# GpSimd's additions to the output wait for one more event of TensorE: the transposes behind the held-weight up product

## What is computed

```python
confidences = sigmoid(einsum('bsh,eh->bse', x, conf_w) + conf_b)
top_bids, selected_experts = top_k(confidences * wealth, 2)
combine = sum(one_hot(selected_experts, 8) * softmax(top_bids)[..., None], axis=2)
g = einsum('bsh,ih->bsi', x, gate_w)        # per expert, i = 1024
u = einsum('bsh,ih->bsi', x, up_w)
expert_out = einsum('bsi,hi->bsh', silu(g) * u, down_w)
output = einsum('ebsh,bse->bsh', expert_out, combine)
x = x + tanh(g_ffn) * output
```

## Time and profile before

| | |
|---|---|
| median of 3 runs | 1449.71 us |
| the profiled execution | 1448.41 us |
| its span, first to last instruction | 1446.8 us |
| mean granted TensorE clock | 0.987 of full speed |
| TensorE busy (matmul) | 1358.9 us, 94% |
| VectorE, ScalarE busy | 1018.4 us, 933.8 us |
| chain that ended last | TensorE 36% of the span, DMA 2% |

### The profile page before, as it was taken

How to read it: one execution, slowest core, us unless ns; L and a number is a source line. 1 busy time by engine, 2 the same in 40 slices (tenths; PEclk the granted TensorE clock), 3 DMA queues, 4 the chain that set the end, 5 groups by cost and what they waited for, 6 DMA issues and landing times. The chain is left out here.

```text
span 1446.8 us, 41651 instructions
## 1 busy us (share of the span) xinstructions
PE 1358.9 (94%) x13880; PEld 971.7 (67%) x13880; DVE 1018.4 (70%) x2553; ACT 933.8 (65%) x1940; POOL 485.5 (34%) x655
## 2 busy tenths in 40 slices
PE   2999999999999999999999958999999999999996
PEld 1466666666666666666666646887777787777774
DVE  4688888888888888888888875666546663444442
ACT  5677878787887878787887765666656553333331
POOL 4423232433433333434432143333344333222221
PEclk9999999999999999999999968999999999999998
DMA  4010101111111101111100335433376743221461
GB/s 118 27 41 26 42 26 36 41 40 47 39 48 32 54 30 45 42 33 54 38 28 21 114 112 156 115 96 90 87 207 185 234 138 89 32 34 31 118 201 16
DMA packets 54867, 107.16 MB, mean 74 GB/s; under 512 B 10833, under 2 KB 32721, under 8 KB 54673
## 3 DMA queue, kind: packets, MB, share of 16 engines
q0 software_dynamic: 23712, 55.71, 14.9%
q1 hardware_dynamic: 30112, 47.75, 10.5%
q10 hardware_dynamic: 848, 1.07, 0.3%
HBM read 69.16 MB, written 35.34 MB: 72 GB/s over the span
## 5 line engine op out<-in xcount | busy, mean ns | idle before, releaser
L875 ACT ACTIVATE sg<-gP,consts 128x512 f32<-128x512 f32 x126 | 86.5, 686 | 242.9 <-PE uP L1436 242.5
L1353 DVE SCALAR_TENSOR_TENSOR act_h<-uP,consts,sg 128x512 f32<-128x512 f32 x126 | 94.5, 750 | 207.5 <-ACT sg L875 207.1
L1436 PE MATMUL fP<-zTs,ws 128*128 128x112 f16 (+1 forms) x1536 | 221.1, 294 | 7.8 <-DVE zTs L1320 5.2
L987 DVE CUSTOM_DVE_ANT_0 ms<-simP,madd,sim_undo 112x488 f32<-112x488 f32 x256 | 184.0, 719 | 5.0 <-remote 2.5
L1436 PE MATMUL fP<-ws,zTs 128*128 128x512 f16 x768 | 186.8, 379 | 0.5 <-DVE kT L977 0.2
L733 ACT ACTIVATE pr<-ms,nmax 112x488 f32<-112x488 f32 x256 | 179.0, 699 | 4.6 <-DVE nmax L987 1.5
L993 DVE SCALAR_TENSOR_TENSOR pT<-ptP,pT 122x448 f16<-122x448 f32 x256 | 157.5, 615 | 28.8 <-ACT pT L740 28.0
L1436 PE MATMUL yP<-W,aT 128*128 (+1 forms) x1512 | 175.4, 273 | 1.7 <-DVE aT L1359 1.7
L1436 PEld LDWEIGHTS fP<-zTs,ws 128*128 128x128 f16 x1536 | 109.8, 99 | 99.6 <-issue 36.8
L1436 PEld LDWEIGHTS yP<-W,aT 128*128 128x128 f16 x1512 | 147.6, 98 | 33.0 <-issue 3.3
L740 ACT ACTIVATE pT<-ptP 122x448 f16<-122x448 f32 x256 | 137.8, 538 | 41.2 <-PE ptP L1494 37.7
(11 more groups left out here) (220 smaller groups left out, 2502.7 us busy)
## 6 DMA issues: line engine op xcount, KB each, us to landing
raw<-wffn POOLq DMA_DIRECT2D x36, 512.0 KB, 6.1
split_experts<-W POOLq DMA_DIRECT2D x12, 1024.0 KB
W<-split_experts SPq DMA_DIRECT2D x16, 768.0 KB
xc<-ctxt SPq DMA_DIRECT2D x32, 375.0 KB
xt<-routed_rows POOLq DMA_DIRECT2D x63, 129.0 KB, 2.5
raw<-wffn SPq DMA_DIRECT2D x12, 512.0 KB, 5.3
xl<-x SPq DMA_DIRECT2D x32, 112.0 KB
xres<-x SPq DMA_DIRECT2D x32, 112.0 KB
```

What stands on the lines that cost most here:

```text
L875: nc.scalar.activation(sg[i][:, :], gP[i][:, :], ACT.Silu, scale=constant(place, 0)).then_inc(s_silu, 1)
L987: nc.vector.tensor_tensor_reduce(out=ms[h % 2][:, :], in0=simP[h % 2][0:S, 0:NK], in1=madd[p][:, :], scale=sim_undo[0:S, 0:1], scalar=3.0e ...
L1353: nc.vector.scalar_tensor_tensor(out=act_h[i][:, :], in0=uP[i][:, :], scalar=constant(place, 2), in1=sg[i][:, :], op0=ALU.mult, op1=ALU.mu ...
L1436: last = nc.tensor.matmul(o, lhs(k, a), rhs(k, c), start=n == 0, stop=n == len(todo) - 1)
```

## The change

One more wait in `add_tile`, between the wait for ysb and the addition. For every tile but the last, the addition of tile t also waits for the transposes of the second half of the activation of tile t + 1 (turned(t + 1, 1) is t + 2, the count of s_at behind them). These come in TensorE's tile t + 2, right behind the up product with weights held; ysb of tile t is written at the beginning of the same tile t + 2.

```diff
@@ -619,6 +619,8 @@
             def add_tile(t, k):
 
                 pool.wait_ge(s_yw, t + 1)
+                if t < NT - 1:
+                    pool.wait_ge(s_at, turned(t + 1, 1))
                 apart(pool)
                 pool.indirect_dma_start(out[:, :], bass.IndirectOffsetOnAxis(ap=xt[k][:, D:D + 1].bitcast(I32), axis=0),
                                         ysb[t % 2][:, :], None, compute_op=ALU.add).then_inc(s_add, 16)
```

## The result

The changed kernel takes 1472.29 us in the median of 4 runs (1470.16 to 1474.61), against 1450.22 for the kernel before (4 runs), a ratio of 1.0162 [1.0149, 1.0176]: 22 us longer. Lines of kernel.py behind the edit stand two further down (L623 is L625 now, L875 is L877).

The account below looks back on a forecast made before the run. TensorE was taken to lead nearly always in the expert stage. 18.3 us for the late power plus 7.4 for raw pieces, 25.7, on the profiled 1448.41 gave 1474.1; the median being 1.3 higher, 1475 us was forecast, range 1461 to 1486.

Parts of the forecast that it names:

- Size and sign: Whole kernel: slower, by 25.7 us, to 1475 us; 0.88 for slower by over 0.2%.
- The addition 2.7 us later: GpSimd's addition in tile 11 would start at 971.98 instead of 969.26, behind the transposes.
- Plain tiles and tail cost nothing: Tiles without raw pieces or a power, and the end, hide the wait entirely: cost 0.
- First cost: Power for the next expert's scale, 2.7 us late, delays the silu and lengthens tiles: seven experts, 18.3 us.
- Squares of pieces 4 and 5 hidden under the power: Late squares one tile before the late power overlap with it; the pair costs the larger, not the sum.
- Second cost: Squares of raw pieces 0 to 2, 2.5 us late, less ScalarE's idle before silu: 7.4 us over six experts.
- The upper bound, neighbours adding (37 us): If late neighbouring tiles added instead of overlapping, the whole cost would be about 37 us.
- The rival of the port: VectorE's two-input residual holds each pair's first raw issue, six times 0.7 us more: 1479 us, chance 0.05.
- The 0.2 us: Moved additions no longer start under VectorE's splits and shorten, making raw pieces 2.5 instead of 2.7 us late.
- GpSimd as the bound: Additions landing after 8.6 us overrun GpSimd's round, 0.6 us in perhaps ten tiles: 1481 us, chance 0.04.
- A faster held-weight product: TensorE's held-weight product speeds up without GpSimd's work beside it, at most 19 us: 1431 us, chance 0.07.
- What the profile would show: Additions 4.4 us into a tile, raw-piece wait up from 21.9 to about 50 us, long tiles twice per expert.

Follow-up runs that it names:

- wait_elsewhere: Kernel before plus the added wait only in steps with nothing urgent queued behind the addition (33 additions); 1446.33 us, ratio 1.0012.
- wait_raw_first: Changed kernel with only the raw issues moved to the head of GpSimd's step, the power left behind; 1462.03 us, 1.0088 of the kernel before.
- wait_before_power: Kernel before plus the added wait only on the seven additions whose landing the power waits for; 1461.80 us, ratio 1.0110.
- wait_power_first: Changed kernel with only the power moved to the head of GpSimd's step, raw issues left behind; 1465.16 us, 1.0094 of the kernel before.
- wait_work_first: Changed kernel with raw issues and power both moved to the head of GpSimd's step; 1439.90 us, 0.9966 of the kernel before.
- later_work_first: Kernel before plus a wait for the tile's second up product, raw issues and power at the step's head; 1454.35 us, ratio 1.0035.
- later_wait: Changed kernel with the wait moved to the end of the tile's second up product; 1554.79 us, 1.0725 of the kernel before.
- before_again: The kernel before, unchanged, run once more for a second trace; 1449.99 us.
- work_first_no_wait: Kernel before, without the added wait, raw issues and power moved to the head of GpSimd's step; 1447.47 us, ratio 0.9985.
- idle_wait: Kernel before plus the same wait instruction for an event one tile earlier, always past, so nothing is delayed; 1449.94 us, ratio 1.0004.
- idle_work_first: Kernel before plus the wait that delays nothing, raw issues and power at the head of GpSimd's step; 1447.77 us, ratio 0.9989.
- wait_before_raw: Kernel before plus the added wait only in the steps that issue raw pieces behind the addition; 1460.74 us, ratio 1.0107.

## Why the prediction was right, and where not

**Size and sign** were right: 1475 forecast, 1472.3 measured, 25.7 us of cost forecast and 25.2 in the trace. That the two agree so closely is in part luck: by the medians the cost is 22.1, against the second trace of the kernel before 23.6, and 3.5 us of it are half clock and -2.4 the plain tiles, both in no step of the sum. Not all of the steps were right either.

- *The addition 2.7 us later*: 4.46 into tile 11 instead of 1.72. Right.
- *Plain tiles and tail cost nothing*: about right, wait_elsewhere 1.0012 [1.0002, 1.0021]. The trace of the changed kernel has tiles 37 to 61 even 2.4 us shorter, which no step had.
- *First cost, 6 x 2.7 + 2.1 = 18.3 for a late power*: the chain was right, the size too large. With the power late alone the pairs grow by 15.0 us in wait_raw_first, of which 1.7 are the half clock of one down product (4.33 instead of 2.62 us to the next start): 13.3, or 1.9 per expert; wait_before_power gives 18.5, of which 2.9 are half clock. The step that failed is "TensorE, busy all through, has no such time to spare". In tile 4 the silu is 2.6 us later than before against the up product, the tile 2.1 longer; in tile 21 it is 1.7 later, the tile 1.2 longer. Some 0.5 us lie between a late silu and a TensorE that stands.
- *Squares of pieces 4 and 5 hidden under the power*: the rule (the larger, not the sum) holds for the pairs together. But the prediction took for granted that the power is the larger. In four of seven pairs the squares are, since they hold TensorE directly, at bP, and not by way of a silu: alone they cost 17.9 us, or 13.1 at full clock, as much as the power. The errors nearly cancel: 20.0 in the pairs (18.2 at full clock), 18.3 forecast.
- *Second cost, 7.4 for pieces 0 to 2*: 8.0 measured in the triples, 0.3, 0.2, 0.6, 1.7, 1.3, 3.9 against 0.7, 1.2, 0.2, 1.8, 2.5, 1.0. As a sum that is right, and by luck: 1.7 of the last 3.9 is half clock, the kernel before is itself 1.9 longer there in its second trace, and with the squares late alone (wait_power_first) the same triples grow by 1.6 only. So the step that gave this term, each late piece less ScalarE's idle before the silu, failed: such pieces alone cost next to nothing. Most of the term comes only when the power is late too; by which path was not tried.
- *The upper bound, neighbours adding (37 us)* falls by the parts' sum of 2.17%, 31 to 33 us, against 22 to 25.
- *The rival of the port*: fallen. In wait_work_first the additions are where the change puts them, beside VectorE's gate, and the time is below the kernel before. In the changed kernel the first raw issue of a pair takes 1.1 to 1.2 us in 16 pairs of 18, as before. 48 of VectorE's 63 residuals with two SBUF inputs (aT from act_h and aT) run beside an addition or a raw issue, and all 63 take 0.68 to 0.69 us. The 45 additions beside one take 1591 ns in the median; so do those of the kernel before that don't start under a split. The 0.2 us was real: 19 additions started under a split before (1829 ns), 6 after, and the median fell from 1646 to 1605. The Trainium skill (SBUF — State Buffer, section "Who interferes with whom") says that a VectorE instruction with two SBUF inputs contends with a GpSimd instruction that reads SBUF; for GpSimd's DMA issues beside these residuals no row here shows that.
- *GpSimd as the bound*: fallen; its busy share stays at 33%, the latest landing is 8.3 us.
- *A faster held-weight product*: a small part is true, as told below, 2.4 us of the 19 it could have been.
- *What the profile would show*: long tiles in two places per expert, as forecast. The wait for raw pieces was forecast at about 50 us and is 62.1: 2 to 3 us of later issue for each piece, but 23 waits instead of 18.

**In a sentence:** the wait costs what GpSimd has queued behind the waiting addition, raw issues and the power, and nothing by itself. That is shown, from both sides: another order takes the cost away with the wait in place, and the instruction without its effect costs nothing. How the cost divides into half clock, pairs and triples is read from single traces.

## What to carry to other kernels

Before you add a wait to an engine that only issues transfers, list what stands behind it in program order, and put what others need soon ahead of it; here that turned a loss of 1.6% into a gain of 0.3% (0.15% by the order without the wait, on another chip). The head of the next round is still behind the wait of this one: a wait long enough reaches it, as in later_work_first. Two late things in neighbouring tiles cost about the larger of the two, so mending one alone looks half useless (0.9% left of 1.6% each time): mend both before you judge. And look for the in-order instruction of the busiest engine that meets the late data first (bP here); it is a shorter way to a stall than the chain that the eye follows.

## What the runs showed of the hardware that was not expected

**The clock can fall after a short idle.** In tile 9 of the changed kernel TensorE's granted clock was 1.00 before an idle of 1.80 us and fell to 0.50 some 0.3 us into the down product behind it (24 matmuls, 4.62 instead of 2.78 us). After idles of 1.97, 2.02, 2.41 and 2.58 us (tiles 4, 23, 33 and 28) of the same execution it stayed at 1.00, so the length of the idle alone doesn't tell. In later_wait such stretches are nearly a third of what its profiled execution lost.

**Plain tiles come in two lengths.** Tiles 37 to 55 sum to 167.2 us in the trace of the kernel before and to 165.6 in that of the changed one. The waits of that stretch, first before (1199.6 to 1366.9 us), then after (1227.2 to 1392.9), are nearly the same. The difference is in the held-weight up product: up to the next start it takes 1.57 us in the mean before and 1.49 after, 19 times 0.08, and every other group of matmuls is equal. ScalarE's silu starts 0.24 us behind its modelled end before, 0.14 after.

```profile
ACT sg L875 <- PE uP L1436: 111.3, 38, 5.1
```

```profile
ACT sg L877 <- PE uP L1438: 109.7, 38, 4.9
```

On the chip of the second group before_again and work_first_no_wait show 167.3 and 167.1, wait_power_first and wait_raw_first 165.6 and 165.7. On that of the third group idle_wait and idle_work_first show 167.5 and 167.3, the two with a wait that bites 165.5 and 165.6. That looks like an effect of where the additions stand in these tiles, under the held-weight up product or behind it. Against it: on the first chip wait_before_raw and wait_before_power, whose additions stand at the old place in these tiles (1.71 us into them), show 165.8 and 165.7, and the other two there 165.6 and 165.8; but no trace of the kernel before was taken on that chip, where it is itself 5 us faster than on the others. Whether the place of the addition, the chip or something earlier in the program sets the length there stays open, and with it how much of wait_work_first's 0.34% is the order's (0.15% by itself, on another chip) and how much the wait's.
